# Attention pooling: the weighted sums behind the fourth group, all four groups split, ScalarE takes the relu of two, natural tiles loaded two chunks behind

## What is computed

```python
W_b, W_c = (fc1_w[:E], fc1_w[E:])
h = jax.nn.relu(jnp.einsum('bse,eh->bsh', behavior_emb, W_b) + (candidate_emb @ W_c)[:, None, :] + fc1_b)
scores = jnp.einsum('bsh,h->bs', h, fc2_w[:, 0]) + fc2_b[0]
attn = jax.nn.softmax(scores, axis=-1)
user_interest = jnp.einsum('bse,bs->be', behavior_emb, attn)
x = jnp.concatenate([user_interest, candidate_emb], axis=1)
z = jax.nn.relu(x @ mlp1_w + mlp1_b)
logit = (z @ mlp2_w + mlp2_b)[:, 0]
```

## Time and profile before

| | us |
|---|---|
| median of 3 runs (lowest, highest) | 282.52 (282.26, 283.63) |
| profiled execution, its time | 283.16 |
| its span | 281.4 |
| TensorE (PE) busy | 269.7, 96% |
| VectorE (DVE) busy | 241.9, 86% |
| ScalarE (ACT) busy | 152.1, 54% |
| GpSimd (POOL) busy | 28.8, 10% |
| moved from memory | 105.83 MB, mean 376 GB/s |

### The profile page before, as it was taken

The page is one execution under the profiler, slowest core; times in us unless marked ns, Lnnn a source line. Parts: engine busy times, 40 slices in busy tenths (PEclk is TensorE's granted clock), DMA queues, the critical chain, the costliest instruction groups (busy, mean ns, idle before and its releaser), DMA issues.

```text
span 281.4 us, 8325 instructions
## 1 busy us (share of the span) xinstructions
PE 269.7 (96%) x2934; PEld 190.7 (68%) x2934; DVE 241.9 (86%) x405; ACT 152.1 (54%) x397; POOL 28.8 (10%) x38
## 2 busy tenths in 40 slices
PE   5987998999999999999999999999999999999896
PEld 5655665767766776767766776767766776767563
DVE  1598879999999999999999999999999999999451
ACT  4365536665555556665555556665555556664312
POOL 2001101111111011111111011111111011111100
PEclk9599999999999999999999999999999999999999
DMA  7999999999999999999999999999999999970000
GB/s 236 436 428 427 423 417 430 425 420 428 429 420 431 426 424 431 424 424 433 422 426 431 424 426 429 426 424 428 428 426 428 422 429 428 424 306 0 2 3 0
DMA packets 10505, 105.83 MB, mean 376 GB/s; under 512 B 1152, under 2 KB 1664, under 8 KB 2432
## 3 DMA queue, kind: packets, MB, share of 16 engines
q1 hardware_dynamic: 10352, 105.39, 89.1%
q10 hardware_dynamic: 144, 0.31, 0.4%
HBM read 105.70 MB, written 0.00 MB: 376 GB/s over the span
## 4 chain that ended last, share of the span: by engine, by line
PE 83%; DMA 11%; issue 2%; DVE 1%; SPq 1%; ACT 1%; DVEq 0%; ACTq 0%
PE s_ps L583 15%; PE u_ps L593 15%; PE z_ps L562 14%; PE z_ps L566 13%; PE z_ps L570 11%; PE z_ps L567 11%; DMA xt<-in_behavior_t 11%; PE z_ps L593 1%; SPq L224 1%; ACT xh L296 1%; PE u_ps L621 1%; PE z_ps L662 1%; PE z_ps L656 1%; PE z_ps L642 0%; DVE hidden L428 0%
## 5 line engine op out<-in xcount | busy, mean ns | idle before, releaser
L428 DVE TENSOR_TENSOR hidden<-z_ps,neg_bias 128x800 f32<-128x800 f32 x96 | 94.5, 988 | 9.7 <-PE z_ps L570 6.3
L418 DVE TENSOR_TENSOR xl<-xt,xh 128x800 fp32r<-128x800 f32 x96 | 94.7, 987 | 4.7 <-ACT xh L296 4.7
L296 ACT CAST xh<-xt 128x800 fp32r<-128x800 f32 x96 | 81.0, 860 | 13.1 <-DMA xt<-in_behavior_t 11.7
L566 PE MATMUL z_ps<-xh,w_hi 128*128 128x512 f32 x192 | 75.6, 394 | 2.9 <-DVE hidden L428 2.9
L567 PE MATMUL z_ps<-xh,w_lo 128*128 128x512 f32 x192 | 63.9, 348 | 0.0
L593 PEld LDWEIGHTS u_ps<-x,weights_by_row 128*32 128x32 f32 x1500 | 46.5, 110 | 12.3 <-issue 12.3
L570 PE MATMUL z_ps<-xl,w_hi 128*128 128x512 f32 x192 | 51.3, 349 | 0.0
L583 PE MATMUL s_ps<-hidden,f_col 128*1 128x384 f32 (+1 forms) x512 | 49.6, 505 | 1.6 <-issue 1.4
L265 POOL TENSOR_TENSOR weights_by_row<-weights,first_sb 128x400 f32<-128x400 f32 x31 | 26.9, 869 | 235.6 <-ACT weights L306 235.6
L593 PE MATMUL u_ps<-x,weights_by_row 128*32 128x128 f32 x1500 | 50.8, 273 | 0.0
L562 PE MATMUL z_ps<-xt,first_sb 128*128 128x288 f32 (+1 forms) x128 | 48.3, 500 | 0.0
(11 more groups left out here) (71 smaller groups left out, 100.9 us busy)
## 6 DMA issues: line engine op xcount, KB each, us to landing
x<-in_behavior SPq DMA_DIRECT2D x32, 1600.0 KB, 13.9
xt<-in_behavior_t SPq DMA_DIRECT2D x31, 1600.0 KB, 15.3
xt<-in_behavior_t SPq DMA_DIRECT2D x4, 400.0 KB, 5.4
first_sb<-in_first ACTq DMA_DIRECT2D x1, 307.5 KB, 4.5
later_sb<-in_later SPq DMA_DIRECT2D x1, 258.5 KB, 19.2
cand<-in_candidate SPq DMA_DIRECT2D x1, 192.0 KB, 5.3
cand<-in_candidate SPq DMA_DIRECT2D x1, 64.0 KB, 4.4
out_logit<-logit SPq DMA_DIRECT2D x1, 1.8 KB
```

The lines of the kernel that those rows point to most:

```text
L296: nc.scalar.copy(xh[g][:, :], xt[q][:, g, :]).then_inc(xh_made, 1)
L418: nc.vector.tensor_tensor(xl[g][:, :], xt[q][:, g, :], xh[g][:, :].bitcast(F32), ALU.subtract).then_inc(xl_made, 1)
L428: nc.vector.tensor_tensor(hidden[q % 2][:, g, :, :].rearrange("p t (b s) -> p t b s", s=PARTS), z, nb.to_broadcast([P, TILES, EACH, PARTS] ...
L566: nc.tensor.matmul(z[:, a:b], w_hi[:, :], xh[g][:, a:b], start=True, stop=False)
```

## The change

Five things change together. Group 3 is split like the others, so there are four `xh` and `xl` tiles. ScalarE makes the hidden values of groups 1 and 3, VectorE those of 0 and 2. On TensorE the scores stay behind group 1 and the weighted sums go behind group 3. The transfers of `x` go one place back in SP's order (`x` of chunk c-2 behind `xt` of chunk c), and an `xt` buffer is free when its last `xl` is made. The third and fourth step of the softmax work on 4 row maxima in place of 32. The core of the diff:

```diff
-PHASE_AT = 1
+SCORES_AT = 1
+SUMS_AT = 3
...
+            def load_transposed(c, buf):
+                if buf is None:
+                    buf = c
+                else:
+                    sp.wait_ge(xl_made, (c + (1 - XT_BUFS)) * GROUPS)
+                sp.dma_start(xt[buf][:, :, :], behavior_t[c, :, :, :]).then_inc(xt_loaded[buf], 16)
+            def load(c, buf):
+                if buf is None:
+                    buf = c
+                else:
+                    sp.wait_ge(pooled_done, c + (1 - X_BUFS))
+                sp.dma_start(x[buf][:, :], behavior_v[c, :, :]).then_inc(x_loaded[buf], 16)
...
             with sp.Fori(0, CHUNKS // X_BUFS - 2) as turn:
                 for j in range(X_BUFS):
-                    sp.wait_ge(z_done, (c + (1 - XT_BUFS)) * GROUPS)
-                    sp.dma_start(xt[j][:, :, :], behavior_t[c, :, :, :]).then_inc(xt_loaded[j], 16)
-                    sp.wait_ge(pooled_done, c - X_BUFS)
-                    sp.dma_start(x[before][:, :], behavior_v[c - 1, :, :]).then_inc(x_loaded[before], 16)
+                    c = turn * X_BUFS + (2 * X_BUFS + j)
+                    load_transposed(c, j)
+                    load(c - 2, (j + 2) % X_BUFS)
...
             def period(c, q, phase):
...
+                if phase == 0:
+                    positive_bias(0)
+                    biased_relu(c, q, 1, phase)
+                    bias_times_f2()
+                    positive_bias(1)
+                    biased_relu(c, q, 3, phase)
+                    for g in range(GROUPS):
+                        next_half(g)
+                    return
                 flush = phase >= 2 and (q - 2) % 2 == 1
                 next_half(0)
+                biased_relu(c, q, 1, phase)
                 next_half(1)
                 if flush:
                     copy_pooled4(c - 2, u_ps)
-                if phase >= 1:
-                    exponents(c - 1, (q + 1) % 2, phase <= 2)
+                exponents(c - 1, (q + 1) % 2, phase <= 2)
                 next_half(2)
-                biased_relu(c, q, phase)
+                biased_relu(c, q, 3, phase)
                 if flush:
                     copy_pooled_t(c - 2, u_ps)
+                next_half(3)
...
                 if step == 3:
+                    op = nc.vector.tensor_reduce(row_max_t[:, :],
+                                                 part_max_t[:, :].rearrange("p (b s) -> p b s", s=PARTS),
+                                                 axis=AX.X, op=ALU.max)
...
                 biased_max(c, q, 0, phase < 2)
-                biased_max(c, q, 1, phase < 2)
+                low_half(c, q, 3)
...
             def products(c, q, g, early):
-                if g == SPLIT:
-                    for a, b in halves:
-                        op = nc.tensor.matmul(z[:, a:b], w_b, xt[q][:, g, a:b], start=True, stop=True)
-                    op.then_inc(z_done, 1)
-                    return
...
-                    if g == PHASE_AT and phase >= 1:
+                    if g == SCORES_AT and phase >= 1:
                         score(c - 1, (q + 1) % 2, phase == 1)
-                    if g == PHASE_AT and phase >= 2:
+                    if g == SUMS_AT and phase >= 2:
                         weighted_sum(c - 2, (q + 2) % X_BUFS)
```

More of the change, by code:

```diff
@@ L19 @@
 GROUPS = P // Q
-SPLIT = GROUPS - 1
+HALF = GROUPS // 2
 EACH = Q // PARTS
@@ L77, in attention_pooling_kernel @@
         xt = [sb(f"xt{i}", [P, GROUPS, WIDTH]) for i in range(XT_BUFS)]
-        xh = [sb(f"xh{i}", [P, WIDTH], F32R) for i in range(SPLIT)]
-        xl = [sb(f"xl{i}", [P, WIDTH], F32R) for i in range(SPLIT)]
+        xh = [sb(f"xh{i}", [P, WIDTH], F32R) for i in range(GROUPS)]
+        xl = [sb(f"xl{i}", [P, WIDTH], F32R) for i in range(GROUPS)]
         hidden = [sb(f"hidden{i}", [P, GROUPS, TILES, Q]) for i in range(2)]
@@ new lines, in _ @@
+            load_transposed(1, None)
+            for c in range(2, X_BUFS):
+                load_transposed(c, None)
+                load(c - 2, None)
+            sp.dma_start(later_sb[:, :], later).then_inc(later_loaded, 16)
+            for c in range(X_BUFS, 2 * X_BUFS):
+                load_transposed(c, c - X_BUFS)
+                load(c - 2, None if c - 2 < X_BUFS else c - 2 - X_BUFS)
+            with sp.Fori(0, CHUNKS // X_BUFS - 2) as turn:
+                for j in range(X_BUFS):
+                    c = turn * X_BUFS + (2 * X_BUFS + j)
+                    load_transposed(c, j)
+                    load(c - 2, (j + 2) % X_BUFS)
@@ L246, in _ @@
+            load(LAST - 1, X_BUFS - 2)
+            load(LAST, X_BUFS - 1)
             for part, (a, b) in enumerate(PART_CHUNKS):
@@ L327, in positive_bias, with biased_relu @@
                 nc.scalar.mul(bias[:, a:b], neg_bias[:, a:b], -1.0).then_inc(bias_made, 1)
-            def biased_relu(c, q, phase):
-                act.wait_ge(z_done, c * GROUPS + GROUPS)
-                if phase <= 1:
+            def biased_relu(c, q, g, phase):
+                act.wait_ge(z_done, c * GROUPS + (g + 1))
+                if phase <= 1 and g == 1:
                     act.wait_ge(bias_made, 1 + phase)
-                if phase >= 2:
+                if phase >= 2 and g == 1:
                     act.wait_ge(scores_done, c - 1)
-                z = z_view(q, GROUPS - 1)[:, 0:WIDTH].rearrange("p (t r) -> p t r", r=Q)
+                z = z_view(q, g)[:, 0:WIDTH].rearrange("p (t r) -> p t r", r=Q)
                 for b in range(EACH):
                     mine = slice(b * PARTS, (b + 1) * PARTS)
-                    op = nc.scalar.activation(hidden[q % 2][:, GROUPS - 1, :, mine], z[:, :, mine], ACT.Relu,
-                                              bias=bias[:, bass.ds(c * ROWS + (GROUPS - 1) * EACH + b, 1)])
+                    op = nc.scalar.activation(hidden[q % 2][:, g, :, mine], z[:, :, mine], ACT.Relu,
+                                              bias=bias[:, bass.ds(c * ROWS + g * EACH + b, 1)])
                 op.then_inc(relu_made, 1)
@@ L448, in softmax @@
                 if step == 3:
-                    each = part_max_t[:, :].rearrange("p (b s) -> p b s", s=PARTS).unsqueeze(2)
-                    op = nc.vector.tensor_reduce(row_max_wide[:, :].rearrange("p (b s) -> p b s", s=PARTS),
-                                                 each.to_broadcast([P, EACH, PARTS, PARTS]), axis=AX.X, op=ALU.max)
+                    op = nc.vector.tensor_reduce(row_max_t[:, :],
+                                                 part_max_t[:, :].rearrange("p (b s) -> p b s", s=PARTS),
+                                                 axis=AX.X, op=ALU.max)
                 if step == 4:
-                    op = nc.vector.transpose(row_max[:, :], row_max_wide[:, :])
+                    op = nc.vector.transpose(row_max[:, :].rearrange("p (b s) -> p b s", s=PARTS),
+                                             row_max_t[:, :].unsqueeze(2).to_broadcast([P, EACH, PARTS]))
                 if step == 5:
```

41 lines of the change are left out of this document (11 added, 30 removed).

## The result

The changed kernel takes 301.15 us (median of 4 runs, 298.39 to 302.0), the kernel before 282.62 in the same session (4 runs, 282.26 to 283.63): a ratio of 1.063, with a 95% interval from 1.056 to 1.071. It is slower, as forecast, within the range of 285 to 303, and 4 us above the 297 that the prediction gave.

What follows compares the result with a forecast made beforehand. TensorE was taken as the bound, the DMA 3% away. A start of 45.1 us and 234.1 for 14 pairs gave 279.2, the last scores 281.7, the span 296.1, the median 297 us; range 285 to 303.

Steps and rivals of the forecast that it cites:

- A period without a flush: TensorE's four groups, scores and sums by starts: 7.87 us, the split's 0.28 eaten by extra changes of width.
- The flush: Behind an odd period's sums, TensorE waits for ScalarE's copy, then transposes: 0.95 us to the next product, before 0.20.
- What is queued behind the copy: ScalarE's late queue frees scores 3.36 us after T (TensorE could go on behind odd period's sums): a wait of 0.06.
- VectorE's chain: VectorE's work behind ScalarE's last cast ends at 9.92 us, TensorE wants its tile at 10.04: fits by 0.12.
- A pair: Two periods on TensorE, one of them flushed: 16.72 us against 15.82 before, 0.90 more.
- The start: Time until TensorE could go on behind period 3's sums: 45.1 us, 3 us lost, 42 to 46 allowed.
- The end: From the last scores, at 281.7, to the span's end: 14.64 as before, less 0.22 in the last softmax: 296.1.
- The transfers: `xt` comes 3.85 us earlier, unused at the start; `x` later at no cost; DMA near 392 GB/s in the middle.
- Rival 1: Changes of width on TensorE partly hidden by early weight loads, only the flush costs: pair 16.0, 287 or 284 us; chance 0.20.
- Rival 2: ScalarE or VectorE becomes the bound, side chains late by 0.7 a pair: 10 us more, 307; chance 0.12.
- Rival 3: Faster: earlier `xt` moves the start to 38.2, TensorE follows the DMA at 15.38 a pair: 271.5 us; chance 0.08.
- Rival 4: No difference: a pair of 15.7 with the forecast start, by accident of the two; chance 0.05.

Runs made afterwards that it cites:

- e9: e5 with ScalarE's copy of the transpose moved ahead of the exponents: 288.11 us, ratio 1.019 to the kernel before.
- e1: The changed kernel with the weighted sums back beside the scores, behind group 1: 278.96 us, ratio 0.986 to the kernel before.
- e6: The kernel before with only the weighted sums moved behind group 3: 305.49 us, ratio 1.080.
- e2: The changed kernel with TensorE's transpose of the sums moved behind group 0 of the next period: 301.59 us, ratio 1.064 to the kernel before.
- e3: The changed kernel with ScalarE's copy of the sums moved behind the hidden values of group 3: 310.28 us, ratio 1.094 to the kernel before.
- e5: The changed kernel with sums copied behind the last cast, transposed behind the next period's group 2, that transpose copied behind the exponents: 298.09 us, ratio 1.052.
- e4: The changed kernel with the edits of both e2 and e3: 292.5 us, ratio 1.034 to the kernel before.
- e7: e1 with ScalarE's first two casts of chunk 1 ahead of group 3's hidden values in period 0: 276.06 us, ratio 0.974 to the kernel before.
- e8: e1 with the transfers in the old order (`x` of chunk c-1 behind `xt` of chunk c): 278.32 us, ratio 0.986 to the kernel before.
- e10: e7 with the transfers in the old order (`x` of chunk c-1 behind `xt` of chunk c): 276.45 us, ratio 0.978 to the kernel before.

## Why the prediction was right, and where it was off

The sign and the mechanism held; by its own steps:

- *A period without a flush*: 7.87 forecast, 7.91 measured. The price of the borders between widths, which the prediction read off, is now measured by itself: 0.33 a period (e9 against e1), where its sums gave 7.87 - (7.81 - 0.28) = 0.34. The split saves 0.24, not 0.28 (e6): a split group among others costs 1.09 to 1.10, and I had worked out 1.08 from a 0.11 that I took for one change of width. The 7.87 does not use that figure.
- *The flush*: 0.95 forecast, 0.78 measured (146.27 to 147.05). The terms are 0.15 to the copy, 0.27 for it, 0.14 to the transpose's matmul, 0.22 to the next product. The step that was mis-sized is the transpose: I added 0.14 from the copy's end and then 0.24 from the weight load to the matmul, and in the trace its first load starts at 146.80 and the matmul at 146.83, both within 0.14 of the copy's end. Against these 0.24 too much stand 0.08 too little for the next product, 0.22 and not 0.14.
- *What is queued behind the copy*: from T to the scores 3.36 forecast, 149.66 - 146.27 = 3.39 measured. It was to cost a wait of 0.06 and costs 0.23 (149.43 to 149.66), since TensorE was ready 0.14 earlier than I had it (3.16 behind T, not 3.30) and the scores came 0.03 later. The errors in the flush and in this wait cancel: a flushed period costs 1.00 more than an unflushed one, 0.98 by the sum. e2 shows that this second chain is as long as the first; the prediction named it. That its price came out right is in part luck: the hidden values end at 3.15 and not at 3.26, because the cast takes 0.75 from start to start and not 0.84, and the scores follow them by 0.24 and not by 0.10. VectorE's chain, which was to fit by 0.12, releases no wait of TensorE in the middle.
- *A pair*: 16.72 forecast, 16.82 measured.
- *The start*: T of period 3 at 45.1 forecast, 43.76 + 1.65 = 45.4 measured, but not by the steps I gave. The first cast of chunk 1 came at 17.86, 0.8 earlier than forecast, and group 1 of chunk 1 at 21.71; what these gained, the half clock from 21 to 27 us took back. That the clock could fall there was not in the sum. The hit is luck in a second way: in e2, e3, e5 and e9, whose order up to there is that of the kernel after, T of period 3 is at 47.1 to 47.3, outside my 42 to 46, because TensorE ran longer at the lower clock at the very start (last section); only e4, which left it as early as the kernel after, has 45.4. e7 confirms the step that mattered, the casts behind the second set of hidden values.
- *The end*: the last scores at 281.7 forecast, 283.14 measured, which is the start's 0.3 and 14 times 0.09 for the pairs, less 0.1 in the wait itself. From there to the end I took 14.42 and it is 16.26: here too the clock had fallen, and the scores alone took 1.24 more. The term "the end" is the largest error, 1.8 of the 3.3 us by which the span was missed (296.1 against 299.4). The rest of the 4 us on the median is the 0.64 by which I put the median below the profiled run; it lies 0.06 below.
- *The transfers*: 392 GB/s forecast for the middle, 404 measured over it, since the DMA ran at 425 until 110 us, and only the last third shows the 388 of a DMA that waits for buffers. That the earlier `xt` is worth nothing, as the sum had it, e8 and e10 show with the sums beside the scores only, and to within 1 to 2 us.

Rival 1 (only the flush costs) has fallen, by e9: the borders cost 9 of the 22 us between the kernel after and e1. Rival 2 (ScalarE's queue becomes the bound) is true in small: it takes 0.2 us in each flush. Rival 3 (faster) needed exactly what e1 restores: with the sums beside the scores TensorE's work is lighter, the DMA stands at its 15.38 a pair, and the kernel is faster than before. Rival 4 (no difference, a pair of 15.7) is excluded by the 16.82. What of the run-to-run spread of the kernel after (298.4 to 302.0) is due to the clock was not settled: its runs' mean clocks, 0.988, 0.983, 0.983 and 0.972, fall as their times rise from 298.39 over 301.1 and 301.21 to 302.0, but only one of them has a trace.

## What to carry to other kernels

A result that one engine finishes, a second copies and the first takes up again needs independent work on the first between its two parts, and the second engine's queue behind the waiting copy is a chain of its own that must be checked too: covering one of the two alone gained nothing (e2), and moving the copy behind work that waits for something later made it worse (e3), as the same slip with the second copy made e5 5.6 us slower than e4. Blocks of matmuls that use the same narrow tiles belong side by side; each extra block of them cost 0.33 us here, more than the 0.24 that a faster form of a product saved. When a change bundles a gain with a loss, take the pieces apart before dropping it: all of this change but one constant, with the first two casts of chunk 1 moved ahead, is 2.6% faster than the kernel before.

## What the runs showed of the hardware that was not expected

The granted clock fell to its lower level (1.2 of 2.4 GHz, 0.50 in the stretch 21 to 27 us) after waits of 2.22 and 1.26 us with 1.7 us of matmuls between them, and stayed there while TensorE was busy for 5.3 of 6 us. At the end it fell behind the waits of 0.50 and 1.45. The kernel before has a wait of 1.38 ahead of its last scores too, with TensorE otherwise busy, and keeps the full clock, 1.55 for those scores. e6, with 0.50 and 1.44, has them at 2.16.

The clock also differs between profiles in the first 15 us. The same two matmuls, first in the kernel after, then in e1:

```profile
10.75 0.91 PE L702 MATMUL u_ps<-cand_t,first_sb 128*128 128x384 f32 x2 [0.57 <-ACT cand_t L304]
```

```profile
11.06 1.65 PE L702 MATMUL u_ps<-cand_t,first_sb 128*128 128x384 f32 x2 [0.57 <-ACT cand_t L304]
```

The clock column reads 1.00 in both from 7 to 14 us, so it is the durations that tell. The first scores of the kernel after start 1.95 us ahead of e1's (23.97 and 25.92), although both have the same order up to there. The lead is the clock's: 0.31 at the rows above, it has grown to 1.90 at the third group of products (12.60 and 14.50), for which e1 still takes 0.63 a matmul of 512 columns and the kernel after 0.40. What sets the moment of the rise no run here shows.
